# Rows of the last two sequences put across in one unit and split in the next, first weights loaded early, statistics two tiles a unit, in a hybrid block on Trainium2

## The reference, cut to what matters

```python
x = x + attn_b(layernorm(x))      # 32 query heads, 8 key/value heads of 128
# in attn_b, b = 8, s = 256:
q = rmsnorm(q, q_norm_w); k = rmsnorm(k, k_norm_w)
scores = einsum('bkgqd,bksd->bkgqs', q, k) / sqrt(HD)
bias = where(rel > 0, -1e30, slopes * rel)
attn = softmax(scores + bias); out = einsum('bkgqs,bksd->bkgqd', attn, v)
return out @ Wo.T
```

## Time and profile before

| what | value |
|---|---|
| time, median of 3 runs | 2485.14 us (2483.37 to 2485.74) |
| time of the profiled execution | 2486.68 us |
| its span, first to last instruction | 2485.4 us |
| PE busy | 2391.3 us, 96% of the span |
| DVE, ACT, POOL busy | 1654.6, 1191.4, 799.2 us |
| mean granted TensorE clock | 0.982 of full |
| one load of `xs`, one of a `qw` set | 1792 KB, 768 KB |
| one load of output weights (two a group) | 512 KB |

### The profile page before, as it was taken

One profiled execution on the slowest core, in us unless ns is written; L12 is line 12 of the kernel. 1 busy time (PEld: TensorE's weight loads), 2 busy tenths in 40 slices (PEclk: granted clock), 3 DMA queues, 4 the chain that ended last, 5 costly groups with the idle time before them and its releaser, 6 DMA issues. The chain is left out here.

```text
span 2485.4 us, 40856 instructions
## 1 busy us (share of the span) xinstructions
PE 2391.3 (96%) x12810; PEld 2040.0 (82%) x12810; DVE 1654.6 (67%) x3959; ACT 1191.4 (48%) x3786; POOL 799.2 (32%) x1204
## 2 busy tenths in 40 slices
PE   6899999999989899999999999999999979999999
PEld 4577777888778798989989889888999867887887
DVE  7666665434367678778777777777777776565554
ACT  6433332223256566666666666666666552122112
POOL 4541343212134244444443444444334340011000
PEclk9799999999989899999999999999999989999999
DMA  4235558898730534534446345354252214555554
GB/s 142 96 132 190 193 209 299 329 372 327 293 130 31 204 136 166 208 141 164 185 166 233 115 166 208 143 199 156 101 204 90 81 64 174 198 203 179 191 191 153
DMA packets 86579, 444.85 MB, mean 179 GB/s; under 512 B 9496, under 2 KB 16664, under 8 KB 66656
## 3 DMA queue, kind: packets, MB, share of 16 engines
q1 hardware_dynamic: 85008, 440.78, 47.5%
q10 hardware_dynamic: 1360, 1.46, 0.2%
HBM read 342.59 MB, written 99.61 MB: 178 GB/s over the span
## 5 line engine op out<-in xcount | busy, mean ns | idle before, releaser
L772 PE MATMUL psum<-qw,xs 128*128 128x384 f32 x2688 | 515.5, 342 | 9.2 <-issue 8.2
L772 PEld LDWEIGHTS psum<-qw,xs 128*128 128x128 f32 x2688 | 465.8, 190 | 10.5 <-issue 9.1
L2385 POOL TENSOR_SCALAR prob<-prob,rsum 128x128 f32<-128x128 f32 (+1 forms) x512 | 227.0, 459 | 637.6 <-DVE rsum L2483 632.8
L2331 ACT ACTIVATE prob<-biased,nmax 128x256 f32<-128x256 f32 (+1 forms) x512 | 227.5, 447 | 142.7 <-DVE nmax L2473 142.2
L772 PE MATMUL psum<-wo_h,oT_h 128*128 128x512 f32 x512 | 213.2, 416 | 3.0 <-ACT stage L946 3.0
L772 PE MATMUL psum<-wo_l,oT_h 128*128 128x512 f32 x512 | 201.5, 393 | 0.0
L772 PE MATMUL psum<-wo_h,oT_l 128*128 128x512 f32 x512 | 201.2, 393 | 0.0
L2292 ACT ACTIVATE squares<-cc 128x128 f32<-128x128 f32 x512 | 152.7, 302 | 62.5 <-DVE cc L2431 51.7
L2458 DVE TENSOR_TENSOR cc<-cc,rr 128x512 f32<-128x512 f32 x64 | 97.8, 1528 | 103.7 <-POOL rr L2375 103.7
L2375 POOL TENSOR_TENSOR rr<-ss,mneg_half 128x6 f32<-128x6 f32 (+1 forms) x128 | 150.4, 1175 | 10.7
L772 PE MATMUL psum<-xT0h,wgu 128*128 128x512 f32 x448 | 152.0, 399 | 0.0
(11 more groups left out here) (318 smaller groups left out, 5889.2 us busy)
## 6 DMA issues: line engine op xcount, KB each, us to landing
xs<-weff_x SPq DMA_DIRECT2D x62, 1792.0 KB, 7.6
wgu<-weff_gu SPq DMA_DIRECT2D x42, 1024.0 KB, 7.6
weff_q<-q_parts SPq DMA_DIRECT2D x56, 768.0 KB, 4.0
qw<-weff_q SPq DMA_DIRECT2D x56, 768.0 KB, 8.2
wD<-weff_dn SPq DMA_DIRECT2D x56, 512.0 KB, 4.7
wS<-weff_s SPq DMA_DIRECT2D x28, 1024.0 KB, 6.8
wdn<-weff_dn SPq DMA_DIRECT2D x42, 512.0 KB, 4.1
weff_gu<-wgu SPq DMA_DIRECT2D x14, 1024.0 KB, 4.6
```

The costliest lines, as they stand in the source:

```text
L772: ins = pe.matmul(out_ap, stat[a], mov[b], start=start and n == 0, stop=stop and n == last)
L2331: act.activation(prob[:, b, lo:hi], biased[:, b % 2, lo:hi], ACT.Exp, bias=nmax[:, b, t:t + 1], scale=-1.0, accum_out=esum[:, b, t:t + 1]) ...
L2385: pool.tensor_scalar(prob[:, b, lo:hi], prob[:, b, lo:hi], rsum[:, b, t:t + 1], 1.0, ALU.mult, ALU.mult).then_inc(prob_done, 1)
```

## The change

- Sequence 6 is put across (`arow`, `axT`, `aev`, `acomb`) in iteration 3 and split (`ahi`, `alo`, `asv`) in iteration 4; sequence 7 in iterations 4 and 5. The split is cut into three pieces at `set0`, `rows` and `set1`.
- The transposes go to bank 4 (`KV`) and bank 5 (`QB[0]`), which the projections of the same iteration have left after the sums `c11` and `c21`; `kT` and `qT0` of the iteration wait for the copies out of them. On PE they stand after `pr3` (new place `rows`) and after `at1`.
- Sequence 7 gets its own `xf2` and `xt2`, laid over `qt2` and `q_parts2`, which are first used in group 1.
- `xs[1]` and the seven `qw` buffers change places in memory, so that all seven sets are loaded ahead of `phase1_over`; `xs[1]` is loaded after it.
- `ln` steps: four tiles in iteration 0 (two at `set0`, two at `set1`), `inv` at `sums` of iteration 1; at the end two tiles an iteration in iterations 57 to 60.

```diff
         def sequence_bank(q, j):
-            return spare(("axT", q, j)) if q < SEQS1 else WO
+            return spare(("axT", q, j)) if q < SEQS1 else (KV, QB[0])[j]
...
+        def sequence_pieces(q, dst, j):
+            f, t = sequence_memory(q)[0:2]
+            if j == 0:
+                return [(dst[:, 6 * P:10 * P].rearrange("p (t k c) -> p t k c", t=2, k=KC // 2), t[:, 0:2, :, :])]
+            if j == 1:
+                return [(dst[:, 0:4 * P].rearrange("p (k c) -> p k c", k=KC), f[:, 0, :, :])]
+            return [(dst[:, 10 * P:].rearrange("p (t k c) -> p t k c", t=2, k=KC // 2), t[:, 2:4, :, :]),
+                    (dst[:, 4 * P:6 * P].rearrange("p (k c) -> p k c", k=KC // 2), f[:, 1, KC // 2:, :])]
...
-                wait_spare(("axT", q, j))
+                pe.wait_ge(c_done, summed(q - 2, ("c11", "c21")[j]))
...
-        xs = [sb2(f"xs{r}", [P, 2, 7, KC // 2, P], F32R) for r in range(2)]
+        xs_first = sb2("xs0", [P, 2, 7, KC // 2, P], F32R)
         qw = [sb2(f"qw{r}", [P, 2, KC // 2, KVQ // 2], F32R) for r in range(7)]
+        xs = [xs_first, sb2("xs1", [P, 2, 7, KC // 2, P], F32R)]
...
-            "pe": "... pr5 pr2 pr4 set0 at0 pr3 pT2 pT3 set1 outa0 at1 outa1 kT0 qT1 qT0 "
+            "pe": "... pr5 pr2 pr4 at0 pr3 rows pT2 pT3 outa0 at1 set1 outa1 kT0 qT1 qT0 "
-            "act": "... exp3 sq5 sq2 rows oThi0 sq4 pThi2 pThi3 sq3 ksc0 oThi1 vhi0 set1 qThi1 "
+            "act": "... exp3 sq5 sq2 oThi0 sq4 rows pThi2 pThi3 sq3 ksc0 oThi1 vhi0 set1 qThi1 "
...
             if where == "set1" and engine == "dve":
-                if u < TPB:
-                    steps.append(("ln", (2, NT - TPB + u), 1))
-                if UNITS - 5 <= u < UNITS - 3:
-                    steps.append(("ln", (3, TPB * (u - UNITS + 5)), TPB))
+                if UNITS - 7 <= u < UNITS - 3:
+                    steps.append(("ln", (3, STILES * (u - UNITS + 7)), STILES))
+            if where in ("set0", "set1") and engine == "dve" and u == 0:
+                first_tile = NT - TPB + (2 if where == "set1" else 0)
+                steps.append(("ln", (2, first_tile), 2))
...
-            fresh = u + AHEAD
+            fresh = u + 3
             if SEQS1 <= fresh < BATCH:
-                steps += {("dve", "set0"): [("arow", fresh, 0)], ("pe", "set0"): [("axT", fresh, 0)],
+                steps += {("dve", "set0"): [("arow", fresh, 0)], ("pe", "rows"): [("axT", fresh, 0)],
                           ("act", "rows"): [("aev", fresh, 0)], ("dve", "rows"): [("arow", fresh, 1)],
-                          ("pe", "set1"): [("axT", fresh, 1)], ("act", "set1"): [("aev", fresh, 1), ("ahi", fresh, 0)],
-                          ("pool", "set1"): [("acomb", fresh, 0)], ("dve", "set1"): [("alo", fresh, 0)],
-                          ("sp", "sets1"): [("asv", fresh, 0)]}.get((engine, where), [])
+                          ("pe", "set1"): [("axT", fresh, 1)], ("act", "set1"): [("aev", fresh, 1)],
+                          ("pool", "set1"): [("acomb", fresh, 0)]}.get((engine, where), [])
+            fresh = u + 2
+            if SEQS1 <= fresh < BATCH and where in ("set0", "rows", "set1") and engine in ("act", "dve"):
+                steps.append(({"act": "ahi", "dve": "alo"}[engine], fresh, ("set0", "rows", "set1").index(where)))
...
-            for j in EARLY_SETS:
+            for j in range(7):
                 load_set(0, j)
-            load_rows(1)
...
                 elif what == "kT":
                     pe.wait_ge(k_sc, a + 1)
+                    if SEQS1 <= a + 2 < BATCH:
+                        pe.wait_ge(a_act, A_ACT["aev", a + 2, 0])
```

More of the change, by code:

```diff
@@ L920, in dve_sequence @@
             else:
-                dve.wait_ge(a_act, A_ACT["ahi", q, 0])
+                dve.wait_ge(a_act, A_ACT["ahi", q, j])
                 _, _, hi, lo = sequence_memory(q)
-                for (h, src), (l, _) in zip(sequence_parts(q, hi), sequence_parts(q, lo)):
+                parts = (sequence_parts(q, hi), sequence_parts(q, lo)) if q < SEQS1 else \
+                    (sequence_pieces(q, hi, j), sequence_pieces(q, lo, j))
+                for (h, src), (l, _) in zip(*parts):
                     ins = dve.tensor_tensor(l, src, h.bitcast(F32), ALU.subtract)
@@ L941, in act_sequence @@
                 act.wait_ge(a_tile, A_TILE["axT", q, j])
-                if q in (0, SEQS1):
+                if q == 0:
                     stack_left(act)
-                else:
+                elif q < SEQS1:
                     act.wait_ge(a_dve, A_DVE["alo", q - 1, 0])
@@ L953, in act_sequence @@
                     act.wait_ge(qkv_mm, len(PRODUCTS2) * (q - 1))
-                for dst, src in sequence_parts(q, hi):
+                for dst, src in sequence_parts(q, hi) if q < SEQS1 else sequence_pieces(q, hi, j):
                     ins = act.activation(dst, src, ACT.Copy)
@@ L972, in sp_sequence @@
         def sp_sequence(q):
-            sp.wait_ge(a_dve, A_DVE["alo", q, 0])
+            sp.wait_ge(a_dve, A_DVE["alo", q, 0 if q < SEQS1 else 2])
             for part in range(2):
@@ L1898, in besides @@
             if where == "set1" and engine == "dve":
-                if u < TPB:
-                    steps.append(("ln", (2, NT - TPB + u), 1))
-                if UNITS - 5 <= u < UNITS - 3:
-                    steps.append(("ln", (3, TPB * (u - UNITS + 5)), TPB))
-            if where == "set1" and engine == "pool":
-                if u == TPB - 1:
+                if UNITS - 7 <= u < UNITS - 3:
[3 more added lines that the diff above has]
+                steps.append(("ln", (2, first_tile), 2))
+            if engine == "pool":
+                if where == "sums" and u == 1:
                     steps.append(("inv", 2, NBLK - 1))
-                if UNITS - 5 <= u < UNITS - 3:
-                    steps.append(("inv", 3, u - UNITS + 5))
+                if where == "set1" and u in (UNITS - 6, UNITS - 4):
+                    steps.append(("inv", 3, (u - UNITS + 6) // 2))
             later_g = g + MADE_AHEAD
@@ L1950, in unit_steps @@
                     yield step_
-        AHEAD = 2
-        EARLY_SETS = [j for j in range(7) if placed[f"qw{j}"] + 8 * SET <= placed["wgu0"]]
         order2 = {e: [] for e in UNIT_STEPS}
-        order2["sp"] += [("lqw", 0, j) for j in range(7) if j not in EARLY_SETS]
+        order2["sp"].append(("lx", 1, 0))
         order2["pool"] += [("rel", 0, 0)]
@@ L2023, in region2 @@
             return psum[:, REGION2[m], 0:KVQ // 2]
-        wo_bank = [e for e in order2["pe"] if e[0] == "axT" or (e[0] == "outa" and e[2] == 1) or (e[0] == "pr" and e[2] == 6)]
+        wo_bank = [e for e in order2["pe"] if (e[0] == "outa" and e[2] == 1) or (e[0] == "pr" and e[2] == 6)]
         def wait_spare(e):
@@ L2031, in wait_spare @@
                 what, a, b = wo_bank[n - 1]
-                if what == "axT":
-                    pe.wait_ge(a_act, A_ACT["aev", a, b])
-                elif what == "pr":
+                if what == "pr":
                     pe.wait_ge(c_done, summed(a, "u2"))
@@ L2213, in load_output_weights @@
                 if g == 1:
-                    sp.wait_ge(a_dve, A_DVE["alo", BATCH - 1, 0])
+                    sp.wait_ge(a_dve, A_DVE["alo", BATCH - 1, 2])
                 elif g > 1 and g - 1 + MADE_AHEAD < KVH:
@@ L2508, in pe_phase2 @@
                     if a in range(SEQS1, BATCH):
-                        pe.wait_ge(a_dve, A_DVE["alo", a, 0])
+                        pe.wait_ge(a_dve, A_DVE["alo", a, 2])
                     else:
@@ L2538, in pe_phase2 @@
                     pe.wait_ge(q_sc1 if b else q_sc0, a + 1)
+                    if b == 0 and SEQS1 <= a + 2 < BATCH:
+                        pe.wait_ge(a_act, A_ACT["aev", a + 2, 1])
                     pe.wait_ge(c_done, summed(a, "c12" if b else "c21"))
```

12 lines of the change are left out of this document (8 added, 4 removed), and 4 rows, old and new, of the table UNIT_STEPS.

## The result

The changed kernel takes 2458.04 us (median of 4 runs, 2457.43 to 2459.4) against 2484.26 for the kernel before (4 runs, 2483.3 to 2485.74) on the same chip: ratio 0.9895, 95% interval 0.9878 to 0.9912, 26.2 us by the medians. The forecast was 2455.3 with a range of 2448 to 2465. The two profiled executions have spans of 2485.4 and 2456.3, 29.1 apart.

What follows compares the result with a forecast made beforehand. PE is busy in 96% of the span, so only its idle and low-clock time can be won. -22.1 + 3.4 - 7.8 - 6.3 + 3.0 = -29.8 from 2485.1 gives 2455.3 us, range 2448 to 2465.

Steps and rivals of the forecast that it cites:

- The start: Start of phase 2: earlier set loads bring `sc0` at 693.4 and not 701.24, 7.8 us less; bounds 7.0 and 9.
- The sequences: Iterations 3 to 6: 22.1 us of idle time and low clock go, 3.4 of added delays come; -18.7.
- The 1.75: Iteration 4: `pT_l` 1.35 us late from sequence 7's rows and sequence 6's piece, plus 0.4 for the second transposes.
- rival 3: Iteration 4: `acomb` on POOL delays the last `alo` on DVE through the port; +1, 2456; a third of forecast's chance.
- the rule: Port pair: a two-input DVE operation in SBUF and a POOL operation reading SBUF exclude each other for a whole instruction.
- The 3.53 are the split itself: Iterations 4 and 5 before: PE's 3.53 us wait on `kTlo0` comes from whole `ahi`, `alo` ahead of `qThi`, `qTlo`.
- The clock: Iterations 3 to 6: with no idle time near 3.5 us left, the low clock goes too; clock 1.00 in them.
- The statistics: `ln` tiles: 6.3 us go at the end; 0.6 comes in each of iterations 57 to 60 and iteration 0, 3.0 together.
- rival 1: Iterations 4 and 5: the split keeps its 3.53 us stall and low clock; 12.5 more, 2468; chance 0.12.
- rival 2: Start of phase 2: earlier loads win only 0 to 3 us, not 7.8; 2460 to 2463; chance 0.10.
- rival 4: Projections: new addresses of `xs[1]` and `qw` lengthen each of 2688 instructions; at 20 ns 2509; chance 0.03.
- rival 5: Iterations 4 to 6: the moved work was not what made them long; gain under 5 us; chance 0.02.

Runs made afterwards that it cites:

- a2_after_again: The changed kernel, unaltered, measured again on the chip of the single-part runs: 2458.69 us, ratio 0.9886 to the kernel before.
- e2_loads_only: The kernel before with only the early loads (seven sets ahead of the end of phase 1, `xs[1]` behind it): 2478.49 us, ratio 0.9965.
- e4_port_wait: The changed kernel with sequence 7's `acomb` on POOL held until sequence 6's last `alo` on DVE ends: 2456.78 us, one run.
- e5_whole: The changed kernel with the split whole again, all three pieces at `set1`, the iteration between rows and split kept: 2456.44 us, one run.

## Why the prediction was right, point by point

- **The start: -7.8 predicted, -8.1 measured** (-7.4 in `a2_after_again`). The step held in its parts. The last product starts 8.9 us after the first (672.73 to 681.59), and the sums-to-scores chain behind its end, 8.2 before, is 8.3 (682.9 to 691.19). `qkw` landed 17.3 us after its issue where it had taken 19.0, and its steps cost nothing: with them out of the way the start is 18.43. `e2_loads_only` has the gain by itself. The clock did not come back for the first scores: PE idles for 2.25 and 1.69 us ahead of the transposes, whose eight then take 2.13 us where a plain iteration has 1.03, and iteration 0 has 0.88, as before.
- **The sequences: -18.7 predicted, -17.6 measured.** Over a plain one, iteration 3 was predicted 1.0 too long and is 0.9 (21.04), iteration 5 was 0.65 and is 0.7 (20.87). Iteration 4 was 1.75 and is 3.0: the term mis-sized. The 1.75 itself holds, since `e4_port_wait` has 21.81, 1.6 above a plain one. The missing 1.2 is the wait for `kT`: its margin was given as 0.5, was 0.3, and DVE came 1.6 late beside POOL. The prediction had this as rival 3 with +1, a third of the forecast's chance, and left it out of its sum. It counted two instructions of DVE as late; it was three, `vlo` too.
- **Its sentence that no row of phase 2 shows the rule for these steps** is true of the moved steps, but another pair showed it. In the kernel before `qsc0` takes 1523 to 1531 ns for all 64 units, beside `qsc1`, where 0.69 us is enough, and I had not asked why. With it, rival 3 would have been a term of the sum.
- **"The 3.53 are the split itself"** names only the end of the chain. ACT idled 3.04 us ahead of `ahi` for POOL's combination, and the whole split without that wait costs 1.05 (`e5_whole`, iteration 5). The forecast did not hang on it, since the change takes away both.
- **The clock: right.** No idle time above 1.2 us is left in iterations 3 to 6, and 6 runs at 1.00. `e5_whole` shows the other side: after 2.23 us without work, an iteration at 0.93 and longer. Where the limit lies no run settles. The waits of 2.09 and 2.08 at the end of iterations 59 and 60 of the kernel before were followed by 1.00 and by 0.92.
- **The statistics: -3.3 predicted, -2.4 measured.** Two tiles cost 0.45 to 0.50 of recorded waiting in each of iterations 57 to 60, 0.6 was predicted. But iteration 57, with a wait at its end alone, is 0.66 over a plain one, iteration 61, with a wait ahead of it alone, 0.16, and 58 to 60, with both, 0.8. The prediction counted a wait once and left out the slower first scores behind it. Iterations 57 to 62 before were 6.3 above six plain ones, as predicted; after, they are 3.2 above where 2.4 was predicted: 0.66, three times 0.8, and 0.16.
- **Rivals 1, 2, 4 and 5 fell.** Waits for `kT` are 1.18 and none, not 3.53; the start won 8.1; `qw,xs` products take 341 ns; `pr1` of unit 1 follows the scores at once (695.52), so `xs[1]` was there; the iterations from which the time was to come gave it.
- **The total.** The terms in the traces sum to -28.1, the spans differ by 29.1, and the medians by 26.2 and 28.8 in two measurements. The forecast of -29.8 gave 1.1 too much for the sequences and 0.9 for the statistics, and 0.3 too little for the start. That is 1.7 of the 2.7 us between 2455.3 and 2458.04; the other 1.0 is within what runs of one kernel differ by.

## What to carry to other kernels

Look first for iterations in which the matrix engine has idle time and ask what stands in front of the instruction that it waits for. Giving that work an iteration of its own between two dependent steps, with other places and banks for its transposes, was worth 14.9 us here, cutting it into pieces 2.7. Where two engines work on one thing side by side, compare each one's duration with that of the same instruction alone: one engine may be faster with both halves, as `qsc` was (1.38 us against 1.53). Look also for waits too short to be marked, in steps that repeat: 0.16 us here, in 50 iterations 7.5. And check that a step is the last to arrive before moving it: the bias steps filled a time in which nothing else could go on.

## What the runs showed of the hardware

- A DVE instruction with two inputs in on-chip memory took longer beside one of POOL: two `alo` 1.03 us alone and 2.08 beside `acomb`, `vlo` 0.42 and 0.96, `qsc0` (128x512) 0.69 and 1.53. That is an addition of 0.5 to 0.8 us for each instruction of DVE, and 0.46 for the one of POOL that was held up.
- An idle time of PE of 1.18 us left the granted clock at 1.00 in the iteration after it (1.00 is the 2.4 GHz level). 2.23 us was followed by an iteration at a mean of 0.93, and 3.53 twice by one at 0.88; about 2.1 us was followed once by 1.00 and once by 0.92 in one trace.
- A wait of 0.45 to 0.50 us of PE cost an iteration 0.66 us ahead of the scores and 0.16 behind them.
- Loads queued one behind the other moved 426 GB/s over 15 us. In their new order they no longer leave PE without work for more than 0.6 us at a time while it has products to make.
